# Two indirect transfers in flight instead of eight, where the second attention fetches its rows back

## The reference

```
x = x + attention0(layernorm(x), ctx, ctx)      # 16 heads of 16 channels
x = x + experts(layernorm(x))                   # 2 shared experts on all rows, 2 of 8 routed ones per row
x = x + attention1(layernorm(x), ctx, ctx)
x = x + sqrt((x' @ cos(theta'))**2 + (x' @ sin(phi'))**2)   # x' = layernorm(x)
```

## Time and profile before

| | |
|---|---|
| median of 3 runs | 1350.27 us (1349.95 to 1350.47) |
| the profiled execution, its own time | 1350.14 us |
| its span, first to last instruction | 1348.3 us |
| TensorE (PE) busy | 1285.6 us, 95% |
| ScalarE (ACT) busy | 1036.6 us, 77% |
| VectorE (DVE) busy | 737.6 us, 55% |
| GpSimd (POOL) busy | 178.4 us, 13% |
| mean granted TensorE clock | 0.976 of full speed |

### The profile page before, as it was taken

The page is one execution under the profiler, slowest core; times in us unless marked ns, Lnnn a source line. Parts: engine busy times, 40 slices in busy tenths (PEclk is TensorE's granted clock), DMA queues, the critical chain, the costliest instruction groups (busy, mean ns, idle before and its releaser), DMA issues. The chain is left out here.

```text
span 1348.3 us, 27233 instructions
## 1 busy us (share of the span) xinstructions
PE 1285.6 (95%) x9750; PEld 611.0 (45%) x9750; DVE 737.6 (55%) x1622; ACT 1036.6 (77%) x1482; POOL 178.4 (13%) x220
## 2 busy tenths in 40 slices
PE   8999999999999999998999999879989999999995
PEld 5422332332333466767999998522223323323322
DVE  5246577577466676446666666633424644443346
ACT  3689999999999754452666666348899999999993
POOL 4111120020020111331000010523300000000000
PEclk9999999999999999999999999868989999999997
DMA  7566744534537060313343452652210110010001
GB/s 222 131 209 219 232 127 152 181 95 155 178 103 265 32 204 17 110 48 102 98 128 114 116 146 79 140 154 70 82 33 1 44 40 1 32 51 1 1 1 62
DMA packets 105889, 140.78 MB, mean 104 GB/s; under 512 B 24916, under 2 KB 77523, under 8 KB 105791
## 3 DMA queue, kind: packets, MB, share of 16 engines
q1 hardware_dynamic: 88368, 102.13, 24.9%
q0 software_dynamic: 9888, 29.76, 7.0%
q10 hardware_dynamic: 7534, 7.57, 2.0%
HBM read 77.11 MB, written 51.69 MB: 96 GB/s over the span
## 5 line engine op out<-in xcount | busy, mean ns | idle before, releaser
L829 ACT ACTIVATE prob<-banks 128x1024 f32<-128x1024 f32 (+1 forms) x832 | 770.4, 1069 | 55.6 <-PE banks L1546 37.8
L1560 PE MATMUL banks<-prob,v 128*32 128x512 f32 (+1 forms) x3328 | 448.6, 611 | 1.1 <-ACT prob L829 1.1
L1546 PE MATMUL banks<-zone,kst 52*128 52x512 f32 (+1 forms) x1664 | 338.3, 470 | 19.0 <-ACT prob L829 17.3
L1546 PEld LDWEIGHTS banks<-zone,kst 52*128 52x128 f32 (+1 forms) x1664 | 138.6, 182 | 363.0 <-ACT prob L829 324.8
L2160 PE MATMUL banks<-xsT_d,w 128*128 128x128 f16 x1776 | 124.7, 220 | 3.2 <-issue 2.9
L1560 PEld LDWEIGHTS banks<-prob,v 128*32 128x32 f32 (+1 forms) x3328 | 65.7, 108 | 130.9 <-issue 108.0
L2160 PEld LDWEIGHTS banks<-xsT_d,w 128*128 128x128 f16 x1776 | 109.6, 98 | 12.6 <-issue 8.9
L2171 PE MATMUL banks<-w,hh 128*128 128x256 f16 x592 | 107.5, 274 | 0.0
L1070 DVE RECIPROCAL late<-late 128x512 f32<-128x512 f32 x31 | 103.9, 3353 | 1.1
L1967 DVE TENSOR_TENSOR hl<-hid,hh 128x128 f16<-128x128 f32 x296 | 83.3, 291 | 32.6 <-ACT hh L1898 24.9
L1065 DVE COPY late<-banks 128x512 f32<-128x512 f32 x31 | 21.4, 690 | 143.9 <-PE banks L1560 124.5
(11 more groups left out here) (270 smaller groups left out, 1281.1 us busy)
## 6 DMA issues: line engine op xcount, KB each, us to landing
weight_parts<-late SPq DMA_DIRECT2D x54, 256.0 KB, 3.3
w<-weight_parts POOLq DMA_DIRECT2D x24, 512.0 KB, 3.8
zone<-q_parts SPq DMA_DIRECT2D x180, 64.0 KB
late<-in_L_ffn_W_r SPq DMA_DIRECT2D x43, 256.0 KB, 4.0
kst<-kparts SPq DMA_DIRECT2D x88, 100.1 KB
q_parts<-qparts SPq DMA_DIRECT2D x16, 512.0 KB, 3.8
weight_parts<-more SPq DMA_DIRECT2D x26, 256.0 KB, 3.2
slot_rows<-late POOLq DMA_DIRECT2D x14, 384.0 KB, 4.2
```

The source lines that it names most:

```text
L829: nc.scalar.activation(prob[0:m, t % P_RING, 2 * (n % 2):2 * (n % 2) + 2, :], score[G % S_RING][0:m, :, :], ACT.Exp, scale=0.25 / WSCALE). ...
L1546: last = nc.tensor.matmul(score[G % S_RING][0:m, a, :], kst[stack, 2 * q + n % 2, t * P:t * P + m].bitcast(F32R), qst[stack, u % Q_RING, n ...
L1560: last = nc.tensor.matmul(outp[u % 2][GROUP * j:GROUP * (j + 1), :], v[0:m, t, u % NQ, j, :], prob[0:m, (u * KT + t) % P_RING, j, :], star ...
```

## The change

The eight gathers of each of the chunks 1 to 3 go through a new helper, `paced_gather`. From the third gather of a batch on, GpSimd waits for the gather two before it to land. For this each chunk has two semaphores instead of one, which its gathers use in turn, and whoever waited for one of them waits for both. Chunk 0's gathers use two semaphores as well but have no waits between them. A path of the program that this input doesn't take (`m_gathered`) keeps its meaning.

```
+IN_FLIGHT = 2
...
-            gathered = [sem(f"gathered{c}") for c in range(NC)]
+            gathered = [[sem(f"gathered{c}_{i}") for i in range(IN_FLIGHT)] for c in range(NC)]
...
-                    gather(pool, back0, 0, n, gathered[0])
+                    gather(pool, back0, 0, n, gathered[0][n % IN_FLIGHT])
+
+            def paced_gather(c, n):
+
+                if n >= IN_FLIGHT:
+                    pool.wait_ge(gathered[c][n % IN_FLIGHT], 16 * (n // IN_FLIGHT))
+                gather(pool, back, c, n, gathered[c][n % IN_FLIGHT])
...
                 for n in range(GATHERS):
-                    gather(pool, back, 1, n, gathered[1])
+                    paced_gather(1, n)
...
                     for n in range(GATHERS):
-                        gather(pool, back, c + 2, n, gathered[c + 2])
+                        paced_gather(c + 2, n)
...
                 for c in range(NC):
-                    pool.wait_ge(gathered[c], 16 * GATHERS)
+                    for signal in gathered[c]:
+                        pool.wait_ge(signal, 16 * GATHERS // IN_FLIGHT)
...
-            def combine(c, source, signal, sums, base):
-                dve.wait_ge(signal, 16 * GATHERS * (1 if signal is not m_gathered else c))
+            def combine(c, source, signals, landed, sums, base):
+                for signal in signals:
+                    dve.wait_ge(signal, 16 * landed)
...
-                    combine(c, back0 if c == 0 else back, gathered[c], added, GATHERS * c)
+                    combine(c, back0 if c == 0 else back, gathered[c], GATHERS // IN_FLIGHT, added, GATHERS * c)
```

More of the change, by code:

```diff
@@ L1011, in _ @@
                     else:
-                        combine(c, back, m_gathered, m_added, GATHERS * (c - 1))
+                        combine(c, back, [m_gathered], GATHERS * c, m_added, GATHERS * (c - 1))
                     statistics(c, g.x, stats, mv, m_stat, 2 * TPC * (c - 1))
```

## The result

The changed kernel takes 1335.07 us (median of 4 runs, 1331.70 to 1336.68) against 1350.11 for the kernel before beside it (1348.03 to 1350.47, 4 runs). The ratio is 0.9888, with an interval of 0.9866 to 0.9910: 15.0 us less. The forecast was 1329 with a range of 1326 to 1355. The direction and the range held; the likeliest case, with its own range of 1326 to 1333, was 6 us too fast. The profiled execution took 1336.68 us, its span is 1334.6.

What follows compares the result with a forecast made beforehand. The prediction took TensorE to bound the kernel, with ScalarE's exponentials nearly as full in the attention loop. From the profiled 1350.14 us, minus 21 for the stalls and plus 0.1 for semaphores, it forecast 1329 us, range 1326 to 1355.

Steps and rivals of the forecast that it cites:

- the likeliest case: Second attention loop: pacing the gathers removes the stalls, giving 1329 us, between 1326 and 1333; chance 0.45.
- What bounds the kernel, and what the three waits are: TensorE carries the chain; ScalarE's three "remote" waits, 14.9 us in all, come from the gather batches of chunks 1 to 3.
- The choice between relief and none: Stalls beside chunks 1 to 3: either gone, -21 us, or kept and lengthened, +3 us; relief was taken.
- The scatters: Expert layer's 32 indirect transfers, one in flight, 527 to 618 us: TensorE never idles, so paced streams don't stall; -21 us.
- two is no great step from three in flight: Gathers of chunks 1 to 3: the stream still doesn't run dry, stalls end 1.7 us later, +3 us in all.
- The relief, 21 us: Attention units 0 to 2: idle time and lower TensorE clock go, 23.3 at most or 22.2 by units, taken as 21.
- The longer batches themselves cost 0; if chunk 2's cover went, under 1 us.: Chunks 1 to 3: each batch some 1.7 us longer (0.5 to 2.9), hidden because rows land before they are needed.
- 12.7 us of cover: Chunk 2: rows landed by 929.4, combined from 942.10; 2 to 3 us left if the loop runs 10 us ahead.
- Waits and semaphores, 0 to 0.1: GpSimd's and VectorE's added waits fall in idle or already met places; the 1.84 us around the span grows 0 to 0.1.
- Stalls that stay: Rival: ScalarE is let go only when a batch has drained, now later; 1353 us, from 1350.5 to 1359; chance 0.33.
- never the gathers: Rival: SyncE's loads beside batches 1 and 3 cause the stalls, so pacing changes nothing; 1350 us; chance 0.07.
- Part of it goes: Rival: stalls become short, or one of three stays; 6 to 14 us gained, 1336 to 1344; chance 0.15.

Runs made afterwards that it cites:

- the second execution of the changed kernel: The changed kernel run again unedited, in the group with the query-split and key-load edits: 1334.46 us, ratio 0.9881.
- the kernel with one stall: The changed kernel with chunk 1's eight gathers issued without waits, only chunks 2 and 3 two in flight: 1336.63 us, ratio 0.9888.
- the two with the masks moved: The changed kernel with four mask loads issued after the third group's key loads: 1330.82 us; the same with the query split before the combination: 1329.17 us.
- 16 semaphores: The changed kernel with four gathers in flight instead of two, on four semaphores a chunk: 1352.42 us, ratio 1.0000.
- the two kernels with GpSimd's own pauses: The kernel before with small GpSimd operations, no landing waits: one pause before each fifth gather, 1337.84 us; one operation before every gather but the first, 1339.07 us.
- kernel with evenly spaced gathers: The kernel before with one small GpSimd operation ahead of each gather of chunks 1 to 3 but the first: 1339.07 us, ratio 0.9917.

## Why the forecast was right in direction and 6 us off

**What bounds the kernel, and what the three waits are.** Right. They belong to the gathers: each batch makes its own (one left unpaced, one stall), and plain transfers make none. One reading was too narrow: the second stall begins at 925.03, just behind the start of the seventh gather (924.98), not with the fifth or sixth.

**The choice between relief and none.** Right. The scatters were the better guide of the two ends: a stream of indirect transfers with pauses does not stall the loop, or only for 1 to 2 us in three of seven profiles with two in flight. Of the two triggers that I left open, "five or six without a pause" holds, and "two is no great step from three in flight" doesn't. Whether that is by the pause or by the number in flight the runs can't say, since at 1.8 us apart there are two in flight anyway.

**The relief, 21 us.** Nearly right. Where lateness is taken away (masks moved) the first four units give 19.0. By unit I had 10.0, 3.4 and 8.8; they gave 7.2, 4.8 and 7.6. Part of that is only where I cut: my stretch for unit 0 ended at 925.60, 3.1 us after its last key tile began, that for unit 1 (953.50) 0.8 us after, so unit 0 was charged with some of unit 1. The rest is what I allowed for units without a stall: 24.5 and 23.5 for units 1 and 2, which take 25.4 and 24.4 at best.

**"The longer batches themselves cost 0; if chunk 2's cover went, under 1 us."** This is the term that failed. It is mis-sized by 2 to 6 us: in the profiles 19.0 minus 14.3, or 2.2 against the second execution of the changed kernel; 5.3 or 3.2 in the kernel with one stall; 3.6 to 5.3 between the median of the changed kernel in the second group and those of the two with the masks moved in the third, 5 to 6 by their ratios. Three readings in it were wrong.

- The batch. I had 1.7 us more (0.5 to 2.9). From first to last start it is 3.2, 2.0 and 3.0 us more in the three batches. And I took the landing of the last gather as fixed. A batch that lasts longer ends among other transfers: in the kernel before the last gather went out 0.7 us ahead of the mask loads (899.32 and 899.99), in the changed one 2.2 us behind their start (902.84 and 900.63), and then took 8.9 us until its data were used, not 3.2. VectorE's wait before chunk 1 grew by 8.9 us (23.63 and 14.73), not by 0.5 to 2.9. I said that no transfer of SyncE waits for the gathers; I didn't ask which ones the gathers would now wait behind.
- The chain. I gave chunk 1 and chunk 2 a cover each, as if they were apart. But chunk 2's batch begins behind chunk 1's combination (`added`), statistics, root and bias. What chunk 1 is late, chunk 2 is too: 9.2 us and then 7.2. The 12.7 us of cover, of which I had left 2 to 3 myself, couldn't bear that.
- The price. "Some tenths" for the late split of a query left out that TensorE then waits and drops to the lower clock: 1.94 us of idling, and unit 2 takes 28.7 us where without the gap it takes 24.4, 4.3 in all.

**Waits and semaphores, 0 to 0.1.** Own time minus span was 1.84 us and is 2.08, so 0.2, a little over the bound. With 16 semaphores it is 2.08 as well (1348.28 and 1346.2).

**The rivals.** Stalls that stay and never the gathers are both ruled out. "Part of it goes" gave 1336 to 1344 (1334 to 1346 where the chances are given) and so comes near the measured time, but by a mechanism that isn't there: in the changed kernel no part of a stall is left. The time alone would have confirmed the wrong one. That 1335 lies within the range of 1326 to 1355 says little, since that range was drawn to cover a slower kernel too.

**Open.** What the indirect transfers hold up between TensorE and those that wait for it, ScalarE and VectorE. The runs show when it occurs (from the fifth to the seventh in a row, 1.25 us apart) and what mostly avoids it, not what it is.

## What to carry to other kernels

When a wait is put down to nothing that the profile knows, look at what else began some us before each of its places: here three unexplained stalls matched three batches of indirect transfers, and spacing them by 1.5 to 1.8 us all but removed them, whether by waiting for a landing or by work between. Don't take the label for the whole: short stalls, and the second one with four in flight, stood under "PE" or "issue", and only the idle times of two engines side by side showed them. When a change makes a batch longer, look up which transfers its tail will now meet, and follow the lateness through what is queued behind it, up to the engine that sets the pace; here a gap of 2 us cost 4 with the clock behind it. And order small loads that touch few partitions behind transfers that somebody waits for.

## What the runs showed of the hardware

- An indirect gather of 128 rows of 1 KB takes 0.95 us of issue. Back to back, 1.25 us apart, five to seven of them stall the loop beside them (by 3 to 6 us of ScalarE in the kernel before); 1.83 us apart, or eight plain transfers of the same size 0.56 us apart (in 4.47), don't. With two in flight, 1.5 to 1.8 us apart on average, four profiles have no stall and three have one of 1 to 2 us.
- Four loads of 50 KB to four partitions delay a gather issued 0.7 to 2.2 us behind their start: 7 to 9 us pass until its data are used, 4.4 where it has only key loads of 100 KB to 16 partitions around it, 3.2 to 3.7 where it goes out just ahead of the masks. In the two kernels with GpSimd's own pauses the last gather goes out 7 and 10 us behind the masks, among the key loads, and still takes 6.3 and 5.6.
- GpSimd's first arithmetic after chunk 1's gathers starts late, by 7.0 to 9.5 us put down to "issue" (9.52 in the kernel before), after one gather as after eight: 7.18 where only one had gone out (kernel with evenly spaced gathers):

```profile
896.94 0.57 POOL L637 TENSOR_SCALAR maskt<-masku 13x128 f32<-13x128 uint8 x1 [7.18 <-issue]
```

- VectorE's eight multiply-adds take 3.76 us, and 4.95 to 6.00 in the executions in which GpSimd's addition of 128x1024 starts in the same stretch (911.36 beside 911.73 in the changed kernel). The Trainium skill (GPSIMD Engine Reference, specifications) says that the two share their way into SBUF, with contention for instructions of VectorE that have two inputs there; the longer times agree.
